# The FFN weights' column masks go from the Vector engine to GpSimd, in place

## What is computed

```python
def _qlinear(qx, scale_x, scale, W, idx, out_idx=None):
    Wr = W[:, idx]
    w_scale = jnp.max(jnp.abs(Wr), axis=1, keepdims=True) / FP8_MAX
    qw = _fp8(Wr / w_scale)
    y = qx * scale_x @ (qw * w_scale).T * scale
    ...
g = _qlinear(qx, sx, sc, w_gate, up_reorder_index, out_idx=down_reorder_index)
u = _qlinear(qx, sx, sc, w_up, up_reorder_index, out_idx=down_reorder_index)
t = jax.nn.silu(g) * u
qt, st, sct = _reorder_quantize_x(t, down_reorder_index)
y = _qlinear(qt, st, sct, w_down, down_reorder_index)
```

## Time and profile before

| | |
|---|---|
| Median of 3 runs | 5517.2 us (5516.86 to 5517.43) |
| The profiled execution | 5517.63 us, span 5515.8 |
| PE busy | 4663.0 us (85%) |
| Vector engine busy | 2823.1 us (51%) |
| Scalar engine busy | 1628.8 us (30%) |
| GpSimd busy | 1530.5 us (28%) |
| Granted TensorE clock in the quantisation stage | 0.50 |

### The profile page before, as it was taken

How to read it: one execution, slowest core, us unless ns; L and a number is a source line. 1 busy time by engine, 2 the same in 40 slices (tenths; PEclk the granted TensorE clock), 3 DMA queues, 4 the chain that set the end, 5 groups by cost and what they waited for, 6 DMA issues and landing times. The chain is left out here.

```text
span 5515.8 us, 209648 instructions
## 1 busy us (share of the span) xinstructions
PE 4663.0 (85%) x93050; PEld 2988.5 (54%) x93050; DVE 2823.1 (51%) x5677; ACT 1628.8 (30%) x3075; POOL 1530.5 (28%) x705
## 2 busy tenths in 40 slices
PE   2599999999999999999998999664356039999996
PEld 1366666666766666666666666464345014444442
DVE  7344434444773444644446444635643865555556
ACT  4122222222222222532226222100000145445443
POOL 0233233314332333033320433043234101111112
PEclk7799999999999999999999999887778569999998
DMA  4211111111111111221113111031133311111111
GB/s 144 92 48 48 48 40 48 48 47 39 48 48 39 48 46 46 70 78 48 47 42 107 43 48 48 25 94 53 51 85 83 124 33 36 38 39 46 39 36 38
DMA packets 223622, 307.24 MB, mean 56 GB/s; under 512 B 39007, under 2 KB 171656, under 8 KB 222666
## 3 DMA queue, kind: packets, MB, share of 16 engines
q1 hardware_dynamic: 217513, 280.04, 17.6%
q10 hardware_dynamic: 3584, 9.44, 0.5%
q0 software_dynamic: 1760, 5.77, 0.3%
HBM read 259.41 MB, written 35.67 MB: 53 GB/s over the span
## 5 line engine op out<-in xcount | busy, mean ns | idle before, releaser
L654 PE MATMUL psum<-whole_w,whole_hot 128*32 128x384 f16 x49152 | 3008.2, 327 | 34.1 <-issue 34.1
L661 PE MATMUL psum<-low_w,low_hot 128*32 128x384 f16 x24576 | 2087.5, 327 | 0.0
L654 PEld LDWEIGHTS psum<-whole_w,whole_hot 128*32 128x32 f16 x49152 | 1352.4, 97 | 690.1 <-issue 37.0
L614 ACT ACTIVATE whole_w<-run_high 32x384 f16<-32x384 f32 x1488 | 776.7, 522 | 2195.5 <-DVE run_high L811 2182.5
L563 POOL TENSOR_TENSOR whole_hot<-whole_a,whole_mask 48x2048 f16<-48x2048 f16 x192 | 692.9, 3609 | 2201.2 <-PE psum L654 1612.9
L811 DVE TENSOR_SCALAR run_high<-psum 128x384 int32<-128x384 int32 x372 | 207.5, 558 | 1603.5 <-PE psum L654 1416.3
L661 PEld LDWEIGHTS psum<-low_w,low_hot 128*32 128x32 f16 x24576 | 676.0, 97 | 326.1
L818 DVE TENSOR_SCALAR whole_w<-psum 32x384 f16<-32x384 f32 x1488 | 822.5, 553 | 27.8
L701 PE MATMUL psum<-low_w,low_hot 64*64 64x384 f16 x12288 | 506.8, 325 | 12.7 <-POOL low_hot L575 7.1
L701 PEld LDWEIGHTS psum<-low_w,low_hot 64*64 64x64 f16 x12288 | 425.8, 108 | 93.7 <-issue 13.6
L575 POOL TENSOR_TENSOR low_hot<-low_a,sum_mask 128x1024 f16<-128x1024 f16 x128 | 242.6, 1895 | 517.3 <-DVE low_a L797 449.4
(11 more groups left out here) (278 smaller groups left out, 3358.3 us busy)
## 6 DMA issues: line engine op xcount, KB each, us to landing
whole_w<-w_rows SPq DMA_DIRECT2D x768, 72.0 KB
low_w<-w_rows SPq DMA_DIRECT2D x384, 144.0 KB
low_w<-w_rows SPq DMA_DIRECT2D x384, 120.0 KB
low_w<-w_rows SPq DMA_DIRECT2D x384, 72.0 KB
low_w<-w_rows SPq DMA_DIRECT2D x384, 48.0 KB
w_rows<-w_split SPq DMA_DIRECT2D x64, 144.0 KB
w_rows<-w_split ACTq DMA_DIRECT2D x64, 144.0 KB
store<-all_states SPq DMA_DIRECT2D x32, 256.0 KB, 2.7
```

The lines of the kernel that those rows point to most:

```text
L614: last = nc.scalar.activation(whole_w[0:Q, buf, u * 2 + half, bq, :], run_high[own, u, :], ACT.Copy, scale=1.0 / HIGH_ONE)
L654: last = nc.tensor.matmul(run[m][u][j * Q:(j + 1) * Q, :], whole_hot[:, buf, sign, kk, j % 2 * Q:(j % 2 + 1) * Q], whole_w[:, buf, u * 2 + ...
L661: nc.tensor.matmul(run[m][u][j * Q:(j + 1) * Q, :], low_hot[:, buf, kk, j % 2 * Q:(j % 2 + 1) * Q], low_w[:, buf, cols(j // 2, u)], start= ...
```

## The change

GpSimd multiplies all 26 pieces by their masks, each in place in `raw_gu` or `raw_dn`, behind its transfers, and signals `masked_ok` for each. The Vector engine's head loses its multiply and begins with the peak, which waits for `masked_ok`. The peak, val and vb read the piece itself. `masked` and the wait for `q_ok` ahead of the mask are gone; the waits for `used_in`, `gathered` and `dn_in` are GpSimd's now.

```diff
-            masked = rows[:, 0:2 * I]
...
+                    pool.wait_ge(gathered, 16 * 2 * KI)
+                    pool.wait_ge(used_in, 16)
+                    for i in range(KI):
+                        for m in range(2):
+                            tile = raw_gu[:, (i + m * KI) * D:(i + m * KI + 1) * D]
+                            nc.gpsimd.tensor_tensor(tile, tile, up_used, ALU.mult).then_inc(masked_ok, 1)
+                    pool.wait_ge(dn_in, 16)
+                    for i in range(KD):
+                        tile = raw_dn[:, i * I:(i + 1) * I]
+                        nc.gpsimd.tensor_tensor(tile, tile, dn_used, ALU.mult).then_inc(masked_ok, 1)
...
-                    v.wait_ge(used_in, 16)
-                    v.wait_ge(gathered, 16 * 2 * KI)
-
-                    def quantise_head(raw, mask, cols, scale_col, m, done, before):
-
-                        need(v, q_ok, before)
-                        nc.vector.tensor_tensor(masked[:, cols], raw, mask, ALU.mult).then_inc(masked_ok, 1)
+
+                    def quantise_head(raw, scale_col, m, done):
+
                         v.wait_ge(masked_ok, done + 1)
-                        nc.vector.tensor_reduce(wmx[:, m:m + 1], masked[:, cols], AX, ALU.max, apply_absolute_value=True).then_inc(wmx_ok, 1)
+                        nc.vector.tensor_reduce(wmx[:, m:m + 1], raw, AX, ALU.max, apply_absolute_value=True).then_inc(wmx_ok, 1)
...
-                    def values(cols, m, done):
+                    def values(raw, cols, m, done):
 
                         a.wait_ge(max_ok, 2 * (done + 1))
-                        nc.scalar.activation(val[:, cols], masked[:, cols], ACT.Copy, scale=wsc[:, m, 0:1]).then_inc(val_ok, 1)
-                        nc.scalar.activation(vb[:, cols], masked[:, cols], ACT.Copy, scale=wsc[:, m, 1:2]).then_inc(val_ok, 1)
+                        nc.scalar.activation(val[:, cols], raw, ACT.Copy, scale=wsc[:, m, 0:1]).then_inc(val_ok, 1)
+                        nc.scalar.activation(vb[:, cols], raw, ACT.Copy, scale=wsc[:, m, 1:2]).then_inc(val_ok, 1)
```

More of the change, by code:

```diff
@@ L1339, in gate_up_tiles @@
                         for m in range(2):
-                            quantise_head(raw_gu[:, bass.ds((i + m * KI) * D, D)], up_used, slice(m * D, (m + 1) * D),
-                                          wcol[:, bass.ds(i + m * KI, 1)], m, 2 * i + m, 2 * i)
+                            quantise_head(raw_gu[:, bass.ds((i + m * KI) * D, D)], wcol[:, bass.ds(i + m * KI, 1)], m, 2 * i + m)
                         for m in range(2):
@@ L1348, in _ @@
                         gate_up_tiles(i)
-                    v.wait_ge(dn_in, 16)
                     with v.Fori(0, KD) as i:
-                        quantise_head(raw_dn[:, bass.ds(i * I, I)], dn_used, slice(0, I), wcol[:, bass.ds(i + 2 * KI, 1)], 0, i + 2 * KI, i + 2 * KI)
+                        quantise_head(raw_dn[:, bass.ds(i * I, I)], wcol[:, bass.ds(i + 2 * KI, 1)], 0, i + 2 * KI)
                         v.wait_ge(qt_ok, 3 * i + 2 * KI)
@@ L1379, in gate_up_tiles @@
                             need(a, q_ok, 2 * i)
-                            values(slice(m * D, (m + 1) * D), m, 2 * i + m)
+                            values(raw_gu[:, bass.ds((i + m * KI) * D, D)], slice(m * D, (m + 1) * D), m, 2 * i + m)
                         for m in range(2):
@@ L1388, in _ @@
                         a.wait_ge(q_ok, i + 2 * KI)
-                        values(slice(0, I), 0, i + 2 * KI)
+                        values(raw_dn[:, bass.ds(i * I, I)], slice(0, I), 0, i + 2 * KI)
                         for c, (o, w) in enumerate(CH):
```

## The result

The changed kernel takes 5528.0 us (median of 17 runs, 5524.1 to 5533.9) against 5517.2 us before (17 runs on the same chips, 5512.3 to 5522.2). The ratio is 1.002 with a 95% interval of 1.0014 to 1.0026: slower by 10.8 us, the interval says by 7.7 to 14.3. The forecast was 5531 with a range of 5525 to 5540.

What follows compares the result with a forecast made beforehand. The Vector engine looked like the bound, but the gate/up loop goes round through Vector and Scalar engines. Removed masks -7.3 us plus waits beside GpSimd's masks +21.2 gave +13.9 on 5517.2: 5531 us, range 5525 to 5540.

Steps and rivals of the forecast that it cites:

- first start: Quantisation stage's start: the first peak waits for GpSimd's mask, 1.27 us plus 0.10 for handing over, not 0.73: +0.64 us.
- first ten turns, without waits: Gate/up loop without Vector masks: first turn 7.26 to 6.88 us (-0.38), nine turns 7.43 to 6.88 (-4.95).
- to the first down piece: First piece of the down weights: the mask's 1.66 us and 0.45 of the tail above leave val's path, -2.11 us.
- three more down pieces, and the last tail: Three later down pieces: val's 0.33 us wait behind the copy shrinks by 0.17 each, -0.51 us.
- waits, tails 0, 1, 2: First three turns' grid, val and q, twice each, wait for GpSimd masks: 5.8, 4.9 and 10.6 us, together +21.2.
- g: Step from the end of the Scalar engine's copy to the next val: taken as 0.16 us, bounds 0 and 0.26.
- sign of being wrong: Gate/up loop: the forecast is wrong if the first turns exceed 14 us, meaning heads are held too.
- Tiny operations held: Rival: a head's 128x1 operations also wait for GpSimd's multiplies, about +18 us, 5535 us; chance 0.12.
- The whole recorded time held: Rival: meetings hold for full recorded times, 1.27 for 1.12 and 0.69 for 0.57: +19.4 us, 5537 us; chance 0.08.
- They do not meet much: Rival: waiting Vector operations get in at once or GpSimd gives way; the 21.2 us shrink, 5510 us; chance 0.08.
- A wait that lasts through GpSimd's queue: Rival: Vector steps are kept out through GpSimd's queue, 5545 us; chance 0.05.
- The better meetings: Rival on how the Vector engine and GpSimd meet, 5527 us, chance 0.09; its details are not in the text given.

Runs made afterwards that it cites:

- after: The changed kernel: all 26 masks moved from the Vector engine to GpSimd, against the kernel before; 5528.0 us against 5517.2, stage 134.7 us against 124.5.
- paced: The changed kernel with GpSimd's masks held back until q of the turn before last is done, long ones likewise to a head each; 5506.8 us, stage 114.0.
- parts: The changed kernel with each short mask cut into 2 GpSimd instructions and each long one into 4; 5522.3 us against 5515.2 before, stage 128.9.
- nomask_memset: The changed kernel without mask multiplications on either engine, GpSimd filling an unused part of rows with zeros 26 times; 5510.4 us against 5516.9 before, stage 116.8.

## Why the prediction was right, and where it was off

By its steps, over the starts of val. "Without waits" is the measured time less the waits read from the timeline.

| term | forecast | measured |
|---|---|---|
| first start | +0.64 | +0.57 |
| first ten turns, without waits | -5.33 (-0.38 and -4.95) | -8.4 |
| to the first down piece | -2.11 | -2.23 |
| three more down pieces, and the last tail | -0.51 | -1.4 |
| waits, tails 0, 1, 2 | 5.8 + 4.9 + 10.6 = +21.2 | 5.7 + 5.2 + 10.7 = +21.6 |
| sum | +13.9 | +10.2 |

**What leaves the path: the mis-sized term is g.** The prediction had the Scalar engine's copy late next, and that is what came. A turn of after that meets nothing, Scalar and Vector engine:

```profile
4428.60 0.69 DVE L1339 SCALAR_TENSOR_TENSOR q<-grid,val 128x512 f16<-128x512 bf16 x1
...
4430.09 1.14 ACT L1375 ACTIVATE qgu<-psum,cnt_s 128x128 f16 x4 [0.52 <-PE psum L1403]
...
4430.35 0.14 DVE L1328 TENSOR_SCALAR wsc<-winv 128x1 f32<-128x1 f32 x1
...
4431.10 0.73 ACT L1368 ACTIVATE val<-store,wsc 128x512 f32 x1
...
4437.68 0.73 ACT L1368 ACTIVATE val<-store,wsc 128x512 f32 x1
```

The second q starts at 4428.60, the copy of its piece 1.49 later and lasts 1.14, and val follows with no wait in its row. The scale was ready at 4430.49; the copy is what val waited for, as predicted. But the copy's record ends at 4431.23 and val starts at 4431.10. So g, the step from the end of the copy to val, is -0.13 us. I took +0.16 from the Vector engine's edge of the same loop and gave 0 as the lower bound. The turn is 6.58 (4431.10 to 4437.68) and not 6.88. This 0.29 counts once in each of the ten turns and in three down pieces: 13 x 0.29 = 3.8 us, as much as the 3.7 us by which the sum is off. What else is off nearly cancels: the waits by +0.4 us, all the rest together by about -0.4. The bound was the mistake. It said that a val can't start before the copy ends by the record, and the earlier trace rows already spoke against it: vb starts at 4381.30 there while val's record runs to 4381.39. With that -0.09 for g the turn would have been put at 6.63. Where nothing holds them, records of instructions in a row overlap on that engine, and I had used such an overlap for GpSimd's queue (0.05) in the same forecast. The gap of 0.26 to 0.37 at the edge was an engine that waited for the scale, and goes away with the wait.

**The down pieces** follow from the same term: their vals start at 4464.51, 4474.77, 4485.09 and 4495.42, 10.3 us apart, where I had 10.6 and the earlier trace rows has 10.8. The step there is the copy's end at 4474.95 against val at 4474.77, so -0.18. The first one's val waits 0.37 for the scale in place of the 2.13 of the earlier trace rows, as forecast.

**The first start** has the hand-over at about 0.02, not 0.10: the mask of 1.27 us and then the reduce 1.29 after the mask's start (4367.53 to 4368.82).

**What comes on the path: right to 2%.** The four meetings of the earlier trace rows gave waits of 0.96, 1.08 and 2.84 to 2.96. The rows of the second and third tails give 0.94 for val and q, 1.06 for the second grid (1.35 less 0.29), and 2.94, 2.83 and 2.83 behind long masks. The release 0.15 us ahead of a mask's recorded end, subtracted from single meetings, held up in fifteen meetings. Paced shows it once more by itself: the grid step of 4374.50 gets going at 4374.50 + 1.14 - 0.29 = 4375.35, 0.13 before the mask's recorded end at 4375.48. For the 0.12 that the prediction takes off a val step on the other side it names no row; the meeting of 5398.81 gives 0.15 (that multiply got going at 5398.98, h ended at 5399.13), and with it the wait is 0.93 where 0.94 was measured. The long mask, estimated at 3.14, is 3.16 undisturbed (the groups of paced). The turns lasted 12.2, 11.8 and 17.3 us where I had 12, 12 and 17.

**Slips in the prediction's text.** It calls the 124.6 us of the earlier trace rows the time to the last transpose; the window ends 0.07 us behind the last q step, and the last transposes end at 4497.3. Nothing was worked out from the difference. By the prediction's own working the lower end for g is -9.4 and not -9.5, and some of the played-through waits are 0.01 to 0.02 too long (0.57 + 1.12 - 0.62 is 1.07, not 1.08); none of it moves the forecast. And its sign of being wrong, first turns over 14 us, contradicts its own third turn of 17; it is a test for the first two alone (12.2 and 11.8). That heads were not held is shown by the 0.15 and 0.67 us of their operations.

**The rivals.** *Tiny operations held* fell: 0.15 at 4381.28 beside running masks, and beside memsets at 4368.59. *The whole recorded time held* fell: a q step behind a val would wait 0.69 + 1.27 - 0.73 = 1.23 us and so last 1.92, and it lasts 1.63. *They do not meet much* fell in the first tail: its six steps wait 5.7 us. A wait that lasts through GpSimd's queue, 5545 in the chances, fell too: in after a waiting step goes ahead of the next queued mask every time, so that val and q last 1.63 us beside short masks, one wait long. *The better meetings*, 5527 in the chances, came nearest in time to the measured 5528.0, and they came by g, which at 0 in place of 0.16 is worth 13 x 0.16 = 2 us. GpSimd's masks were no shorter than forecast (1.27 and 3.16 us undisturbed in paced), and a waiting step got going no earlier: 0.13 us before the mask's recorded end in paced, where the forecast has 0.15.

**What stays open.** In total the kernel lost 10.8 us and the stage 10.2. The rest, 0.6, is within the interval, and I looked for no cause.

## What to carry to other kernels

Before work is moved to an idle GpSimd, list what the Vector engine does in those same microseconds. GpSimd's multiplies cost nothing here beside reduces (0.67 to 0.69 us with and without them), 128x1 operations (0.15) and the Scalar engine's val and vb (0.71 to 0.74 beside the masks in after, 0.73 behind them), and kept each two-input or int16 step of 128x512 out for most of their own length (0.94 us of 1.27, and 2.83 of 3.16). The same masks gave -10.5 us or +10.2 us in this stage, by two waits that decide when they run; where they can't be timed, cutting them shorter takes a part of the loss back (+4.4 in parts for +10.2). And when a wait leaves a loop's edge, the next link has no gap of its own: take the step between two instructions of one engine from a place of that engine where nothing is waited for, which can be below nothing (-0.13 us here).

## What the runs showed of the hardware that I had not expected

- An instruction of the Scalar engine whose wait is already met starts 0.09 to 0.18 us before the record of the one ahead of it ends: 0.13 in the turns after (4431.10 against 4431.23), 0.09 in the turn of the earlier trace rows, 0.18 at the down pieces. It does so across an iteration of the loop as within it.
- A GpSimd memset, which only writes, held back the grid step in nomask_memset (1.20 to 1.28 for 0.29) and left the steps with two inputs alone (0.69).
- The alternation is strict: with GpSimd's queue never empty, each val, each q and each second grid step waits for one GpSimd instruction, and the first grid step of a tail for what is left of one (0.84, 0.34 and 0.24 us in after). None waits for two. Halving the instruction took the wait from 0.94 to 0.40 us, less than half: a part alone lasts 0.72, and by the timetable of the prediction the wait is 0.57 + (0.72 - 0.15) - 0.73 = 0.41.
- GpSimd loses as well: 45.0 us for the 26 masks in after, 40.0 in paced.
